# Row maxima of causal attention: two heads in row halves of the array, at the end of each step

## The chip, the core and the metric

The kernel runs on one core of a Trainium2 chip. The metric is the device time of one execution in microseconds (us), as the median of several runs. TensorE multiplies matrices into PSUM (8 banks of 512 fp32 columns for each of 128 partitions), VectorE and ScalarE read PSUM, GpSimd (POOL) works on SBUF alone, and SyncE (SP) issues most DMA transfers. Each engine works through its own queue in order and waits on semaphores.

## The reference

Two layers over x of shape (8, 1024, 256). A layer normalises x, and adds to x the result of causal attention and that of a mixture of 8 experts, of which each token takes two. In the first layer an expert is two matrices with a ReLU between them, in the second a single matrix, and the gates are normalised there.

```python
xn = _layernorm(x, axis=-1)
x = x + _L0_attn_ref(xn, Wq, Wk, Wv, Wo) + _L0_ffn_ref(xn, W_gate, b_gate, W1, b1, W2, b2)
xn = _layernorm(x, axis=-1)
x = x + _L1_attn_ref(xn, Wq, Wk, Wv, Wo, bo) + _L1_ffn_ref(xn, We, be, Wg, bg)
# attention, 16 heads of 16:
scores = jnp.einsum('bhqd,bhkd->bhqk', q, k) / jnp.sqrt(jnp.asarray(HD, x.dtype))
scores = jnp.where(causal, scores, jnp.asarray(-jnp.inf, scores.dtype))
probs = jax.nn.softmax(scores, axis=-1)
out = jnp.einsum('bhqk,bhkd->bhqd', probs, v)
```

The part at stake is the maximum over a row of scores that softmax subtracts before the exponential.

## The kernel before

The work is cut into 16 runs: one layer of one batch each. Batches go in pairs, so that the experts' tiles of one run can be gathered while the other's attention is computed. A run has 48 steps. A step is one unit of attention: a tile of 128 keys against a block of up to 512 queries, for a set of four heads. A run has 8 sets: 4 groups of heads for the first 512 queries (4 steps each), then for the second 512 (8 steps each). All five engines follow the same program of steps, each with its own function `step(g)`, and the order of calls in these functions is the order of work. Tables of step numbers (`TURN`, `PROJ`, `XT`, `VALUES`, `Y`, `GATES` and others) say at which step of a run, or ahead of it, each of the other parts is done. A run's preparation thus goes on while the run before it is at its attention.

Queries and keys are kept as three bf16 parts each (high, middle, low) and a score is the sum of six products of parts, stacked along the rows of one matmul: 6 x 16 = 96 rows. SP loads these stacks from DRAM (`load_stack`, line 457), for queries into `qs`, for keys into `k_first` (first 512 keys) and `k_second`. Two more rows hold the row maxima of the queries, negated and in two bf16 parts, against ones on the key side, so that the score matmul (`scores`, L1147, 98 rows) subtracts them. ScalarE's exponential (`exponentials`, L722) then reads PSUM and writes `probs`, and the attention product (`attend`, L1210) multiplies `probs` with `v`, four heads side by side in column strips of 32, into the bank `po`.

The maxima come ahead, 12 steps before their set's first use at the earliest: `maxima` (L1160) computes scores again, with queries as rows, in pieces of one head, a tile of 128 queries and up to 512 keys, four pieces in every step (`pieces_of`, `maxima_at`). VectorE's `maximum` reduces each piece: a plain maximum where no key lies in the future (L875), a masked one that also takes in the plain piece's result where some do (L879, followed by a read of its accumulator). When all pieces of a set are read, VectorE splits the maxima into two parts (`split_maxima`, L1042 and L1043), TensorE turns them into rows (`turn_maxima`, L1222), VectorE copies these to `mT` (L1049), and SP moves them into the two rows of `qs` (`load_maxima`, L492). `TURN` says at which step.

Two rings of PSUM banks set who waits for whom. The ring `pmx`, 4 banks, takes the pieces of the maxima, the projections of queries and keys (L1290), the output projection (`Y`, L1249), the turned sets and maxima. The ring `pst`, 3 banks, takes the scores, and around them the tokens of an expert's tile (L1168), its hidden layer (L1179, first layer only), its output (L1194), the values (L1301) and the transposes of xn. Each use of a ring takes the next bank and waits until the use before in that bank has been read (`mx_read`, `st_read`). In TensorE's step a piece of the maxima stands ahead of each score:

```python
                for j in range(GH):
                    for piece in work[j:j + 1]:
                        maxima(*piece)
                    if j == 2:
...
                    if j == 3 and tile_out(g):
                        expert_out(*tile_out(g))
                    if unit(g):
                        scores(*unit(g), j)
                    if j == 0 and tile_hidden(g):
                        hidden(*tile_hidden(g))
```

VectorE's step likewise takes the four pieces one by one, with the statistics, the gates and the rest between them. The experts' tiles go through the steps in twos: tokens in odd steps, the output in the next even one (second layer), or hidden layer in the next and the output in the odd step after it (first layer).

## Time and profile before

| what | value |
|---|---|
| runs | 3080.80, 3087.09 and 3089.62 us, median 3087.09 |
| span of the profiled execution | 3081.5 us |
| TensorE (PE) busy | 2982.1 us, 97% |
| VectorE (DVE) busy | 2421.1 us, 79% |
| ScalarE (ACT) busy | 1972.9 us, 64% |
| GpSimd (POOL) busy | 1191.8 us, 39% |
| mean granted TensorE clock | 0.993 |
| DMA | 473.27 MB, mean 154 GB/s |

The span is the time from the first to the last instruction of the profiled execution; it lies among the runs' times, so that nothing of weight stands around it. Busy time counts the time in which at least one instruction of the engine was under way. Matmuls are pipelined: one lasts longer than the distance to the next start, so for TensorE the distances between starts tell more than the durations.

### The profile page before, as it was taken

What the parts mean: (1) busy time and instruction counts of PE and PEld (TensorE: products, weight loads), DVE (VectorE), ACT (ScalarE), POOL (GpSimd) and SP (SyncE); (2) the same over time, 40 slices, a digit from 0 to 9 for tenths busy, and PEclk for the clock granted to TensorE, in tenths of its full rate; (3) what the DMA queues carried; (4) which work ended last, traced back from release to release, by engine and by line L of the source; (5) the groups of instructions that cost most, each with busy time, mean ns of one, the idle gap of its engine ahead of it and who ended that gap; (6) DMA issues with size and microseconds to landing.
All of it is one profiled execution on the core that took longest, in us unless ns stands there. A gap on an engine that the chain in (4) does not pass through costs nothing.

```text
span 3081.5 us, 62739 instructions
## 1 busy us (share of the span) xinstructions
PE 2982.1 (97%) x19312; PEld 1582.3 (51%) x19312; DVE 2421.1 (79%) x7517; ACT 1972.9 (64%) x4954; POOL 1191.8 (39%) x1424
## 2 busy tenths in 40 slices
PE   6999999999999999999999999999999999999998
PEld 3555545444565554545455555454545556544443
DVE  7777788887777878888777887878888777787884
ACT  2666666666666666666666666666666666666665
POOL 3325234252523525335252342534435243252533
PEclk8999999999999999999999999999999999999999
DMA  5766455363655645446374554635547465453642
GB/s 166 208 180 198 133 152 156 109 191 115 187 170 145 178 136 162 132 123 186 110 211 140 166 165 134 176 110 152 178 117 212 138 176 161 126 164 109 170 137 66
DMA packets 276876, 473.27 MB, mean 154 GB/s; under 512 B 52960, under 2 KB 185792, under 8 KB 274496
## 3 DMA queue, kind: packets, MB, share of 16 engines
q1 hardware_dynamic: 236928, 379.48, 40.9%
q0 software_dynamic: 29952, 81.83, 10.2%
q10 hardware_dynamic: 9664, 7.93, 0.9%
q8 instruction: 159, 2.61, 0.4%
q14 instruction: 173, 1.42, 0.2%
HBM read 344.19 MB, written 130.03 MB: 154 GB/s over the span
## 4 chain that ended last, share of the span: by engine, by line
PE 81%; DVE 10%; issue 4%; ACT 3%; POOL 1%; DMA 0%; ACTq 0%; DVEq 0%; POOLq 0%
PE po L1210 17%; PE pmx L1160 15%; PE pst L1147 13%; PE pst L1194 10%; PE pmx L1290 6%; PE pst L1179 5%; DVE pmx L879 4%; PE pst L1301 4%; PE pmx L1249 3%; PE pst L1168 3%; PE pmx L1228 2%; PE pst L1216 2%; DVE rmax L875 1%; ACT probs L722 1%; ACT oraw L751 1%
## 5 line engine op out<-in xcount | busy, mean ns | idle before, releaser
L722 ACT ACTIVATE probs<-pst 128x512 f32<-128x512 f32 (+3 forms) x3072 | 1401.8, 497 | 413.5 <-PE pst L1147 409.7
L621 POOL TENSOR_SCALAR_AFFINE_SELECT probs<-probs 128x512 f32<-128x512 f32 x512 | 326.7, 638 | 1464.7 <-ACT probs L722 1463.6
L875 DVE TENSOR_REDUCE rmax<-pmx 128x1 f32<-128x512 f32 x1024 | 671.1, 683 | 127.6 <-PE pmx L1160 121.0
L1147 PE MATMUL pst<-qs,k_first 98*128 98x512 bf16 (+3 forms) x2048 | 688.6, 342 | 8.7 <-ACT probs L722 4.3
L1160 PE MATMUL pmx<-k_first,qs 96*128 96x512 bf16 (+2 forms) x2048 | 668.0, 343 | 16.1 <-DVE rmax L879 5.0
L879 DVE CUSTOM_DVE_ANT_0 pmx<-pmx,mask,rmax 128x128 f32<-128x128 f32 (+3 forms) x1024 | 534.5, 555 | 162.7 <-PE pmx L1160 152.9
L1210 PE MATMUL po<-probs,v 128*32 128x512 f32 (+3 forms) x6144 | 657.5, 500 | 4.2 <-POOL probs L621 4.1
L879 DVE CUSTOM_DVE_ANT_0 pmx<-pmx,mask 128x128 f32<-128x128 f32 (+3 forms) x1024 | 483.4, 510 | 125.7 <-PE pmx L1160 124.5
L594 POOL DMA_INDIRECT xg<-xn_rows,rows_of x368 | 357.9, 973 | 95.7 <-issue 51.4
L1160 PEld LDWEIGHTS pmx<-k_first,qs 96*128 96x128 bf16 x2048 | 198.6, 98 | 348.0 <-issue 122.5
L1160 PE MATMUL pmx<-k_second,qs 96*128 96x128 bf16 (+3 forms) x1024 | 304.2, 301 | 17.5 <-DVE otok L1016 8.7
L1147 PE MATMUL pst<-qs,k_second 98*128 98x512 bf16 (+3 forms) x1024 | 300.3, 301 | 3.0 <-ACT probs L722 2.2
L608 POOL DMA_INDIRECT yk<-y_slots,slot x256 | 244.9, 957 | 123.2 <-DVE x L1036 46.3
L1147 PEld LDWEIGHTS pst<-qs,k_first 98*128 98x128 bf16 x2048 | 199.5, 98 | 178.0 <-ACT probs L722 50.7
L879 DVE DVE_READ_ACCUMULATOR2_ANT rmax<- 128x1 f32 x2048 | 288.5, 141 | 0.0
L744 ACT ACTIVATE ys<-pst 128x256 f32<-128x256 f32 x368 | 142.8, 388 | 181.1 <-PE pst L1194 137.4
L1290 PE MATMUL pmx<-xnT,wqk 128*128 128x512 f32 x512 | 247.6, 607 | 7.3 <-DVE rmax L875 6.5
L1210 PEld LDWEIGHTS po<-probs,v 128*32 128x32 f32 x6144 | 121.1, 108 | 219.9 <-issue 171.2
L727 ACT ACTIVATE xgT<-pst 128x256 f32<-128x256 f32 x368 | 142.6, 387 | 119.7 <-PE pst L1168 117.2
L627 POOL TENSOR_TENSOR parts<-rest,parts 128x512 bf16<-128x512 f32 x128 | 148.8, 1163 | 178.1 <-ACT parts L766 178.1
L761 ACT ACTIVATE parts<-pmx 128x512 bf16<-128x512 f32 x128 | 76.4, 597 | 191.8 <-PE pmx L1290 191.8
L1194 PE MATMUL pst<-wt,hT 128*128 128x256 f32 x736 | 194.7, 386 | 3.2 <-ACT probs L722 3.2
(143 smaller groups left out, 3626.4 us busy)
## 6 DMA issues: line engine op xcount, KB each, us to landing
wt<-w_tiles SPq DMA_DIRECT2D x161, 513.0 KB
qk_parts<-parts SPq DMA_DIRECT2D x256, 192.0 KB
y_slots<-ys SPq DMA_DIRECT2D x368, 128.0 KB
wt<-w_tiles SPq DMA_DIRECT2D x184, 256.0 KB
qs<-qk_parts SPq DMA_DIRECT2D x128, 192.0 KB
xn_rows<-xn SPq DMA_DIRECT2D x16, 1024.0 KB, 6.4
qs<-qk_parts SPq DMA_DIRECT2D x128, 128.0 KB
k_first<-qk_parts SPq DMA_DIRECT2D x64, 192.0 KB, 3.8
```

The lines of the kernel that those rows point to most:

```text
L594: pool.indirect_dma_start(out=xg[:, m % XRING], out_offset=None, in_=xn_dram[q % 2], in_offset=bass.IndirectOffsetOnAxis(ap=rows_of[:, q % ...
L608: pool.indirect_dma_start(out=yk[:, m % GRING], out_offset=None, in_=y_dram[q % 2], in_offset=bass.IndirectOffsetOnAxis(ap=slot[:, q % 2, ...
L621: pool.affine_select(out=tri, in_=tri, compare_op=ALU.is_ge, fill=0.0, base=0, pattern=[[0, GH], [1, P]], channel_multiplier=-1).then_inc( ...
L722: act.activation(probs[:, u % 2, j, 0:w], ps[:, 0:w], ACT.Exp, scale=DH ** -0.5).then_inc(st_read, 1)
L875: dve.tensor_reduce(rmax0[:, col:col + 1], src, AX_X, ALU.max).then_inc(mx_read, 1)
L879: dve.tensor_tensor_reduce(out=src, in0=src, in1=mask[:, BANK - (b - a):BANK], op0=ALU.add, op1=ALU.max, scale=1.0, scalar=rmax0[:, col:co ...
L1147: pe.matmul(ps[:, 0:w], keys[0:SROWS, j, k % HT * P:(k % HT + 1) * P], qs[0:SROWS, set_no(q, n) % QRING, j, a:a + w], start=True, stop=Tru ...
L1160: pe.matmul(bk[:, 0:b - a], qs[0:STACK, set_no(q, n) % QRING, j, t % HT * P:(t % HT + 1) * P], keys[0:STACK, j, 0:b - a], start=True, stop ...
L1179: mm = pe.matmul(ps[:, j * P:(j + 1) * P], wt[:, m % WRING, a:a + P], xgT[:, m % 2, k], start=(k == 0), stop=(k == KD - 1))
L1194: mm = pe.matmul(ps[:, 0:D], src[:, m % 2, k], wt[:, m % WRING, a:a + D], start=(k == 0), stop=(k == KD - 1))
L1210: mm = pe.matmul(po[HS * j:HS * (j + 1), BANK - w:BANK], v[:, q % 2, k, col:col + HS], probs[:, u % 2, j, 0:w], start=(k == 0), stop=(u in ...
L1290: mm = pe.matmul(ps[:], wqk[l][:, m, k, tile * P:(tile + 1) * P], xnT[:, k, c * BANK:(c + 1) * BANK], start=(k == 0), stop=(k == KD - 1))
```

## The change

In words:

- `pieces_of`: the pieces of a set are listed in another order, two heads beside each other: head 0 with head 2, then head 1 with head 3, the same queries and keys for both; the tiles of queries in the order 0, 3, 1, 2.
- The stacks lie otherwise in `qs`, `k_first` and `k_second`. The four products of high and middle parts (64 rows) lie in rows 0 to 63 for heads 0 and 1 and in rows 64 to 127 for heads 2 and 3; the two products with low parts and the rows of the maxima lie in what is left. The scores of heads 0 and 1 use 98 rows as before, those of heads 2 and 3 use all 128, of which 30 hold zeros.
- `maxima` takes the 64 rows alone, so it leaves the products with low parts out of the maxima, and the two matmuls of a pair use different halves of the array's rows and different banks.
- TensorE's step: all four pieces come last, after the attention product. Projections, values, transposes of xn and output projection now stand after score 0, in place of score 2's turn. VectorE's step: the pieces come last, too. `TURN` is one step later.
- VectorE: `maxima_pair` takes the plain maxima of a pair in one instruction over two neighbouring banks; where the ring's end lies between the two banks, or where there is a mask, `maximum` takes each alone.
- SP: a stack is loaded with six transfers of 32 rows of 2 KB instead of three of 48, 32 and 16 rows of 4 KB; a part is stored with one transfer instead of two. The maxima's rows go two partitions at a time.
- Some memsets for the rows of ones and zeros at the start, and one part of the gates (`GATE_PLACES`) a step earlier.

The diff, cut to its core:

```diff
+MAIN, REST = 4 * DH, 2 * DH
+SIDES = (0, 1), (2, 3)
+MAIN_AT, REST_AT, MAX_AT = (0, P - MAIN), (MAIN, P - MAIN - REST), (STACK, 0)
+SCORE_ROWS = (STACK + MROWS, P)
...
-    return [(j, t, a, min(a + BANK, (t + 1) * P)) for a in range(0, (c + 1) * BANK, BANK)
-            for j in range(GH) for t in range(c * HT, (c + 1) * HT)]
+    return [(side[i], c * HT + t, a, min(a + BANK, (c * HT + t + 1) * P)) for a in range(0, (c + 1) * BANK, BANK)
+            for i in range(len(SIDES[0])) for two in ((0, 3), (1, 2)) for t in two for side in SIDES]
...
-TURN = [MAX0 + (max(i for i, (m, _) in enumerate(PIECES) if m == n) + 1) // PER_STEP for n in range(NSETS)]
+TURN = [MAX0 + 1 + (max(i for i, (m, _) in enumerate(PIECES) if m == n) + 1) // PER_STEP for n in range(NSETS)]
...
+                for side, heads in enumerate(SIDES):
+                    dst = buf[:, heads[0]:heads[-1] + 1].rearrange("p h t -> p (h t)")
+                    for half in range(2):
+                        row = MAIN_AT[side] + half * 2 * DH
+                        two = (src[side, :, 0:2] if m == 0 else
+                               src[side, :, 1 + half].unsqueeze(1).broadcast_to([DH, 2, len(heads) * BANK]))
+                        sp.dma_start(dst[row:row + 2 * DH], two).then_inc(s, 16)
+                    sp.dma_start(dst[REST_AT[side]:REST_AT[side] + REST], src[side, :, 0:3:2]).then_inc(s, 16)
...
+            def maxima_pair(q, n, k):
+
+                j, t, a, b = pieces_of(n)[k]
+                if k == 0 and q * NSETS + n >= 2:
+                    dve.wait_ge(msplit_ready, q * NSETS + n - 1)
+                dve.wait_ge(mx_full, mx_done("max", q, n, k + 1))
+                first = MX["max", q, n, k] % MXRING
+                two = rmax0[:].rearrange("p (j t) -> p j t", t=HT)[:, j::len(SIDES[0]), t % HT]
+                dve.tensor_reduce(two, mx_banks[:, first:first + 2, 0:b - a], AX_X, ALU.max).then_inc(mx_read, 2)
...
-                pe.matmul(bk[:, 0:b - a], qs[0:STACK, set_no(q, n) % QRING, j, t % HT * P:(t % HT + 1) * P],
-                          keys[0:STACK, j, 0:b - a], start=True, stop=True).then_inc(mx_full, 1)
+                main = slice(MAIN_AT[j // len(SIDES[0])], MAIN_AT[j // len(SIDES[0])] + MAIN)
+                pe.matmul(bk[:, 0:b - a], qs[main, set_no(q, n) % QRING, j, t % HT * P:(t % HT + 1) * P],
+                          keys[main, j, 0:b - a], start=True, stop=True).then_inc(mx_full, 1)
...
             def step(g):
-                work = maxima_at(g)
                 if tile_turned(g):
                     turn_tokens(*tile_turned(g))
                 for j in range(GH):
-                    for piece in work[j:j + 1]:
-                        maxima(*piece)
-                    if j == 2:
+                    if j == 3 and tile_out(g):
+                        expert_out(*tile_out(g))
+                    if unit(g):
+                        scores(*unit(g), j)
+                    if j == 0:
+                        if tile_hidden(g):
+                            hidden(*tile_hidden(g))
...
+                if unit(g - 1):
+                    attend(*unit(g - 1))
+                for piece in maxima_at(g):
+                    maxima(*piece)
```

How this moves instructions. On TensorE, before, around a step of the second layer with unmasked maxima and the end of its set (po is the attention product, pst from qs a score, pmx from qs a piece of the maxima, pst from wt an expert's output, pmx from mparts the turn of the maxima):

```order
L1210 MATMUL po<-probs,v 32x256 x4
L1160 MATMUL pmx<-k_first,qs 128x512
L1147 MATMUL pst<-qs,k_first 128x512
L1160 MATMUL pmx<-k_first,qs 128x512
L1147 MATMUL pst<-qs,k_first 128x512
L1160 MATMUL pmx<-k_first,qs 128x512
L1147 MATMUL pst<-qs,k_first 128x512
L1160 MATMUL pmx<-k_first,qs 128x512
L1194 MATMUL pst<-wt,xgT 128x256 x2
L1147 MATMUL pst<-qs,k_first 128x512
L1222 MATMUL pmx<-identb,mparts 128x128
L1210 MATMUL po<-probs,v 32x128 x4
```

The same step with the change, and the start of the next (L1174 is a score, L1188 a piece of the maxima, L1222 now the expert's output, L1238 the attention product, L1196 the tokens):

```order
L1174 MATMUL pst<-qs,k_first 128x512 x3
L1222 MATMUL pst<-wt,xgT 128x256 x2
L1174 MATMUL pst<-qs,k_first 128x512
L1238 MATMUL po<-probs,v 32x128 x4
L1188 MATMUL pmx<-k_first,qs 128x512 x4
L1196 MATMUL pst<-ident,xg 128x128 x2
```

The three first scores now follow each other, the four pieces stand in a row behind the attention product, and the turn of the maxima has left this step for the next.

On VectorE, before, at the end of a set's pieces (L879 is the masked piece and the read of its accumulator, L1042 and L1043 the split, L875 a plain piece of the next set, L852 and L855 statistics, L1049 the copy of the turned maxima):

```order
L879 ISA pmx,rmax<-pmx,mask,rmax 128x384
L879 ISA rmax 128x1
L879 ISA pmx,rmax<-pmx,mask,rmax 128x512
L879 ISA rmax 128x1
L1042 TENSOR_SCALAR mparts<-rmax 128x16
L1043 SCALAR_TENSOR_TENSOR mparts<-rmax,mparts 128x16
L875 TENSOR_REDUCE rmax<-pmx 128x1 x2
L852 BN_STATS stats<-x 128x6 x2
L855 BN_AGGR mv<-stats 128x2 x2
L875 TENSOR_REDUCE rmax<-pmx 128x1 x2
L1049 COPY mT<-pmx 32x128
```

With the change (L885 the masked piece, L858 and L861 the statistics, L898 a pair of plain pieces, L1065 and L1066 the split, L1034 to L1037 the result of a turned set, L1072 the copy):

```order
L885 ISA pmx,rmax<-pmx,mask,rmax 128x384
L885 ISA rmax 128x1
L885 ISA pmx,rmax<-pmx,mask,rmax 128x384
L885 ISA rmax 128x1
L858 BN_STATS stats<-x 128x6 x2
L861 BN_AGGR mv<-stats 128x2 x2
L898 TENSOR_REDUCE rmax<-pmx 128x2 x2
L1065 TENSOR_SCALAR mparts<-rmax 128x2x8
L1066 SCALAR_TENSOR_TENSOR mparts<-rmax,mparts 128x2x8
L1034 TENSOR_SCALAR osum<-pmx 128x16
L1035 RECIPROCAL osum<-osum 128x16
L1037 TENSOR_TENSOR otok<-pmx,osum 128x4x64
```

The split of a set now stands behind the pieces of the next set's first step, and the statistics ahead of them.

## Rows read from the trace of the kernel before

**Rows 1.** The page, busy times of the engines (us, share of the span, instructions).

```profile
PE 2982.1 (97%) x19312; PEld 1582.3 (51%) x19312; DVE 2421.1 (79%) x7517; ACT 1972.9 (64%) x4954; POOL 1191.8 (39%) x1424
```

**Rows 2.** The page, chain that ended last, share of the span by line.

```profile
PE po L1210 17%; PE pmx L1160 15%; PE pst L1147 13%; PE pst L1194 10%; PE pmx L1290 6%; PE pst L1179 5%; DVE pmx L879 4%; PE pst L1301 4%; PE pmx L1249 3%; PE pst L1168 3%; PE pmx L1228 2%; PE pst L1216 2%; DVE rmax L875 1%; ACT probs L722 1%; ACT oraw L751 1%
```

**Rows 3.** Order of time, TensorE in a dense step: start us, us it lasts, instruction.

```profile
1363.51 0.22 PE L1160 MATMUL pmx<-k_second,qs 96*128 96x128 bf16 x1
...
1364.50 0.38 PE L1160 MATMUL pmx<-k_second,qs 96*128 96x512 bf16 x1
1364.72 0.38 PE L1147 MATMUL pst<-qs,k_first 98*128 98x512 bf16 x1
1365.03 1.06 PE L1210 MATMUL po<-probs,v 128*32 128x512 f32 x8
1366.03 0.23 PE L1160 MATMUL pmx<-k_first,qs 96*128 96x128 bf16 x1
```

**Rows 4.** Groups by line and form, the attention product: count, busy us, mean ns.

```profile
L1210 PE MATMUL po<-probs,v 128*32 128x512 f32 x3072 | 411.7, 608 | 0.1
```

**Rows 5.** Order of time, TensorE and ScalarE in the last run's last steps.

```profile
3034.90 0.82 PE L1147 MATMUL pst<-qs,k_second 98*128 98x512 bf16 x3
...
3036.12 1.10 PE L1194 MATMUL pst<-wt,xgT 128*128 128x256 f32 x4 [0.41 <-ACT probs L722]
...
3049.05 0.82 PE L1147 MATMUL pst<-qs,k_first 98*128 98x512 bf16 x3
...
3049.54 2.07 ACT L722 ACTIVATE probs<-pst 128x512 f32<-128x512 f32 x4 [0.66 <-PE pst L1147]
...
3050.19 0.39 PE L1147 MATMUL pst<-qs,k_first 98*128 98x512 bf16 x1 [0.32 <-ACT probs L722]
```

**Rows 6.** Order of time, tokens of an expert's tile and the first exponential.

```profile
3032.11 0.44 PE L1168 MATMUL pst<-ident,xg 128*128 128x128 f32 x2
...
3032.58 0.38 ACT L727 ACTIVATE xgT<-pst 128x256 f32<-128x256 f32 x1 [0.65 <-PE pst L1168]
...
3032.91 0.60 ACT L722 ACTIVATE probs<-pst 128x512 f32<-128x512 f32 x1
```

**Rows 7.** Groups by line and form, projections.

```profile
L1290 PE MATMUL pmx<-xnT,wqk 128*128 128x512 f32 x512 | 247.6, 607 | 7.3 <-DVE rmax L875 6.5 <-DVE rmax L879 0.2
...
L1249 PE MATMUL pmx<-wo,attn 128*128 128x256 f32 x512 | 129.9, 382 | 0.0
```

**Rows 8.** Stretches: length, busy us by engine, granted clock, DMA share, GB/s.

```profile
1306.00:1350.10 44.10, 41.78 (x247) 19.77 (x246) 37.87 (x114) 24.67 (x59) 13.02 (x15) 0.96 0.40 106
...
3049.00:3060.50 11.50, 9.91 (x65) 2.34 (x62) 4.21 (x9) 9.05 (x20) 7.03 (x8) 1.00 0.24 69
```

**Rows 9.** Order of time, VectorE at four masked pieces and the split.

```profile
3032.64 0.36 DVE L879 CUSTOM_DVE_ANT_0 pmx<-pmx,mask,rmax 128x128 f32<-128x128 f32 x1 [1.71 <-PE pmx L1160]
...
3033.92 0.76 DVE L879 CUSTOM_DVE_ANT_0 pmx<-pmx,mask,rmax 128x512 f32<-128x512 f32 x1
3034.59 0.14 DVE L879 DVE_READ_ACCUMULATOR2_ANT rmax<- 128x1 f32 x1
3034.77 0.17 DVE L1042 TENSOR_SCALAR mparts<-rmax 128x16 bf16<-128x16 f32 x1
3034.97 0.17 DVE L1043 SCALAR_TENSOR_TENSOR mparts<-rmax,mparts 128x16 bf16<-128x16 f32 x1
```

**Rows 10.** Groups by line and form, VectorE's plain maximum.

```profile
L875 DVE TENSOR_REDUCE rmax<-pmx 128x1 f32<-128x512 f32 x1024 | 671.1, 683 | 127.6 <-PE pmx L1160 121.0
```

**Rows 11.** Waits of TensorE's weight loads: us in total, times, longest.

```profile
PEld pmx L1160 <- DVE rmax L879: 119.8, 202, 1.2
...
PEld pst L1147 <- ACT probs L722: 65.2, 181, 0.9
PEld pmx L1160 <- DVE rmax L875: 47.5, 89, 0.8
```

**Rows 12.** Order of time, SP issues the three transfers of a stack.

```profile
1501.81 1.31 SPq L464 DMA_DIRECT2D k_second<-qk_parts  x3
```

**Rows 13.** Waits of SP's queue: us in total, times, longest.

```profile
SPq L525 <- ACT ys L744: 813.2, 208, 8.0
```

More of the change, by code:

```diff
@@ L219, in uses @@
             mx["rows", q] = len(mx)
+        for q, n, k in maxima_at(g):
+            mx["max", q, n, k] = len(mx)
     return mx, st
@@ L1099, in step @@
                     take_rows(q)
+                work = maxima_at(g)
+                for i in range(0, len(work), 2):
+                    if in_pair(*work[i]):
+                        maxima_pair(*work[i])
+                    else:
+                        maximum(*work[i])
+                        maximum(*work[i + 1])
             def order_weights(l):
```

155 lines of the change are left out of this document (70 added, 85 removed).

## The prediction

> **What bounds the kernel now.** I read the page's busy times first, then the chain that ended last, then the order of time in a dense stretch and in the last steps, then the waits. TensorE is busy 97% of the span and VectorE 79% [rows 1]; line L1160, the maxima matmuls, is 15% of the chain, second to the attention product [rows 2]. So TensorE's own queue sets the end, and what counts is how far apart its matmuls start. In a dense step [rows 3] the reader is to see the starts: from the first maxima matmul at 1363.51 to the last score at 1364.72 stand four maxima (128, 256, 384 and 512 columns) and three scores of 512; a 512 takes 0.22 us to the next start, so the four maxima take 1.21 - 3 x 0.22 = 0.55 us. The attention product starts 0.31 us after the last score instead of 0.22, so entering its 32-column strips costs 0.09, and the next matmul starts 1.00 us after it.
>
> There are 16 runs of 48 steps, 768 in all, with four maxima matmuls in each. In 256 steps all four have 512 columns and no mask (4 x 0.22 = 0.88 us), in 512 they are the masked row of rows 3 (0.55): together 225 + 282 = 507 us of TensorE's time.
>
> **The change, part by part.** The sum is made against the profiled span, 3081.5 us; the runs took 3080.8 to 3089.6, with a median 5.6 above the span, which I add at the end. About 0.3% (9 us) is what a measurement of this kernel can tell from no change.
>
> *Pairs.* Two heads' maxima now use rows 0 to 63 and 64 to 127 of the array, one right behind the other, in two banks. No row of before shows two matmuls on different rows. The nearest is the attention product: eight matmuls of 512 columns in 1.00 us [rows 3], though each lasts 0.608 [rows 4]; they run four at a time in four column strips. Bounds: nothing gained, if the halves take turns, or half of 507, 253 us. I take 253, since that row shows tiles at work side by side. The Trainium skill, TensorE: Matmul & The Clock Gate, section Measured speedup vs the span model, gives 3.07 times for four row tiles of 512 columns; an estimate from it for two is 1.53 times, so 176 us, and the sum would be 77 us higher. No run here shows it yet.
>
> *One more change of tiling a step.* The maxima follow the attention product, so the way out of its strips leads into row halves, and a way from these to whole rows is new. Bounds: 0, or the entry's 0.09. I take 0.09 x 768 = 69 us.
>
> *Scores in a burst.* This is the dearest part. Before, a maxima matmul stood between each two scores; now at most an expert's tile does, and the ring pst still has three banks: score 3 needs the bank of score 0, which ScalarE must have read. The last twelve steps of before have no maxima left and show just this [rows 5]: three scores start from 3049.05 on, the fourth could at 3049.71 (3 x 0.22), but the first exponential starts at 3049.54 and the fourth score at 3050.19, 0.48 us late. With the expert's output in fourth place (3034.90, then 3036.12) it is 0.56. With token tiles ahead [rows 6] ScalarE starts the first exponential 0.80 us after the tokens and needs 0.60; the fourth score could start at 0.27 + 3 x 0.22 = 0.93 and starts at 1.40, again 0.47. Only where a projection (247.6 us in 128 steps, 1.9 each) or an output projection (129.9 in 64, 2.0 each) stands between the first two scores [rows 7] is there no wait. That leaves 36 of 48 steps: 576 x 0.48 = 276 us. Bounds: 0.40 each, 230, if steps with values or token transposes between the scores wait less, and 0.56 each, 323. The clock adds nothing: over those bursts the granted clock is 1.00, the 2.4 GHz level [rows 8].
>
> *VectorE later by most of a step.* Its maxima can't begin before TensorE's last matmuls of a step. Four masked pieces take it from 3032.64 to 3034.59, 1.95 us, and the split of the maxima ends 0.55 later [rows 9]. Two unmasked pieces in one instruction cost between one reduce, 0.68, and two, 1.37 [rows 10]; from the masked forms (0.76 for 512 columns, 0.36 for 128 [rows 9], so 1.04 ns a column) I take 0.68 + 0.53 = 1.21. What that saves VectorE in 385 pairs (the ring's end keeps 127 apart) lies in its idle time: 0 on the path. But a finished set's split stands behind the maxima of the next set's first step, so it is ready 2.5 to 2.9 us after TensorE finished those, while TensorE's turn of it (L1222) stands behind the scores alone, some 1.7 us after. In a quarter of the 128 turns nothing else stands between (no expert's output, no set), and TensorE waits some 0.95; in the others some 0.15: 32 x 0.95 + 96 x 0.15 = 45 us. Likewise 64 output projections and 32 projections of layer 1 that follow an unmasked step ask for the first pair's bank 0.3 to 0.6 us after it was written, and it is free after 1.21: 0.6 each, 55 us. Bounds of both together: 0 and 200.
>
> *Waits of before that go.* TensorE's weight loads waited 119.8 and 47.5 us for VectorE's maxima and, at the scores, 65.2 for ScalarE [rows 11]; such a wait is partly covered by the matmul in flight. TensorE's own idle time is 99 us in all (span less busy, [rows 1]), start and end included. Between 60 and 230 I take 110 as lost time that the new order replaces.
>
> *Edits at nothing.* SP issues six transfers per stack instead of three, 768 more at 0.44 each (three in 1.31 us [rows 12]), 340 us, less 128 stores; it waits 813 us for ScalarE at L525 [rows 13], which covers that. Without this cover a stack would come 1.3 us later, and it is loaded several steps ahead. The split's rows reach qs a step later; three steps remain. The wider memsets cost a few us at the start at most.
>
> The sum: -253 + 69 + 276 + 45 + 55 - 110 = +82. From 3081.5 that is 3163.5, and with 5.6 for the median 3169.
>
> **The rivals.**
> *Faster: one wait covers the other.* While TensorE waits for ScalarE in each burst, VectorE catches up; then its waits of before vanish as far as the weight loads' rows say (200 us) and turns and banks cost nothing: -253 + 69 + 276 - 200 = -108, so 2979. For it: VectorE has only 79%. Against it: the waits at turns and banks run from the end of the maxima, whatever came before. It decides from where VectorE's side, waits gone less waits new, reaches 92 us.
> *VectorE becomes the bound.* In the ten steps with the gates (1306.0 to 1350.1) VectorE is busy 37.87 of 44.10 us [rows 8]. If it must stand idle there each time until the step's last matmuls, some 0.6 us in each of 160 steps, 96 us come on top: 3265. Against it: TensorE's steps get longer too. The Trainium skill, TensorEngine Tiling (Array Packing), section PSUM Bottleneck, says that tiling speeds up TensorE but not the emptying of PSUM, which may then be the bottleneck; these rows neither bear it out nor exclude it.
> *The halves take turns.* Then the 253 us aren't gained: 3422. For it: no row shows row halves. Against it: the column strips do run together.
>
> **How the numbers follow.** Forecast 3169, from 3100 to 3240: 0.45. Within 0.3% of before, between it and the faster rival: 0.06. Faster: 0.24. VectorE the bound: 0.15. Halves in turn: 0.10. So faster 0.24, same 0.06, slower 0.70. The range leaves out the halves in turn and the lower part of the faster case, and holds the rest: 2990 to 3300.
>
> **What would show it.** Right: two maxima matmuls that start almost together, and the next pair 0.22 us later; about 0.09 us lost behind them; the fourth score some 0.48 us late, with the exponential named as what ended the wait; small waits at the maxima. Wrong: 0.22 us between all starts of the maxima line (halves in turn), a fourth score on time, or VectorE without idle time in the gate steps.

## The result and the profile after

The changed kernel takes 3384.14 us (median of 4 runs, 3380.42 to 3389.01) against 3085.03 for the kernel before on the same chip: 1.097 times as long, 95% interval 1.0953 to 1.0987. The forecast was 3169, range 2990 to 3300. The direction was right, the size was not.

Lines have moved: maxima L1160 is now L1188, scores L1147 L1174, attention product L1210 L1238, an expert's output L1194 L1222, tokens L1168 L1196, the turn L1222 L1250, set L1228 L1256, projections L1290 L1318, output projections L1246 and L1249 L1274 and L1277; VectorE's plain maxima are L881 (alone) and L898 (pairs), the masked ones L885.

The page of the changed kernel, busy times, then the chain by engine and by line:

```profile
PE 3010.2 (89%) x19312; PEld 1429.6 (42%) x19312; DVE 2349.0 (69%) x7135; ACT 1951.0 (58%) x4954; POOL 1190.3 (35%) x1426
...
PE 68%; ACT 12%; DVE 12%; issue 6%; DMA 1%; POOL 0%; SPq 0%; ACTq 0%; DVEq 0%; POOLq 0%
PE po L1238 16%; PE pst L1222 10%; PE pmx L1188 9%; PE pst L1174 9%; PE pmx L1318 7%; PE pst L1207 4%; ACT probs L731 4%; DVE rmax L898 3%; PE pmx L1277 3%; PE pst L1196 3%; PE pst L1329 3%; DVE pmx L885 2%; ACT xgT L736 2%; PE pmx L1256 2%
```

The chain by engine before was:

```profile
PE 81%; DVE 10%; issue 4%; ACT 3%; POOL 1%; DMA 0%; ACTq 0%; DVEq 0%; POOLq 0%
```

TensorE was busy 97% of a shorter span [rows 1]; now it is 89%, and VectorE and ScalarE have less to do and yet hold a larger part of the chain, ScalarE above all. The maxima have fallen from 15% [rows 2] to 9%. So TensorE waits. The order of time of two steps without sets or projections shows where (start us, us it lasts, instruction; in brackets the engine's idle time ahead of it and what ended it), TensorE first, then ScalarE:

```profile
1490.34 0.45 PE L1188 MATMUL pmx<-k_second,qs 64*128 64x256 bf16 x4
1490.72 0.82 PE L1174 MATMUL pst<-qs,k_first 98*128 98x512 bf16 x3
1491.95 1.10 PE L1222 MATMUL pst<-wt,xgT 128*128 128x256 f32 x4 [0.41 <-ACT probs L731]
1492.89 0.38 PE L1174 MATMUL pst<-qs,k_first 128*128 128x512 bf16 x1
...
1494.19 0.45 PE L1188 MATMUL pmx<-k_second,qs 64*128 64x128 bf16 x4
1494.57 0.44 PE L1196 MATMUL pst<-ident,xg 128*128 128x128 f32 x2
1494.85 1.52 PE L1174 MATMUL pst<-qs,k_first 98*128 98x512 bf16 x4
1496.29 1.07 PE L1238 MATMUL po<-probs,v 128*32 128x512 f32 x8
```

```profile
1491.21 1.57 ACT L731 ACTIVATE probs<-pst 128x512 f32<-128x512 f32 x3 [0.92 <-PE pst L1174]
...
1495.05 0.38 ACT L736 ACTIVATE xgT<-pst 128x256 f32<-128x256 f32 x1 [1.02 <-PE pst L1196]
1495.33 2.06 ACT L731 ACTIVATE probs<-pst 128x512 f32<-128x512 f32 x4
```

The expert's output is due at 1490.72 + 3 x 0.22 = 1491.38 and starts at 1491.95, 0.57 late, because it needs the bank of score 0, whose exponential began at 1491.21. In the next step four scores behind tokens take 1.44 us (1494.85 to 1496.29) to the attention product instead of 0.97, which is 4 x 0.22 and the 0.09 of its strips. Those are the waits that the prediction read from the last steps of before [rows 5, 6].

The row halves do what the prediction expected of them. Four maxima, a pair of 128 and a pair of 512 columns, take 1494.57 - 1494.19 = 0.38 us, where four with the same number of columns in all took 0.55 [rows 3]. Four of 512 take 0.53, from the first here to the tokens behind them, where the prediction counted 0.88 for the kernel before:

```profile
1011.64 0.61 PE L1188 MATMUL pmx<-k_first,qs 64*128 64x512 bf16 x4
1012.17 0.33 PE L1196 MATMUL pst<-ident,xg 128*128 128x128 f32 x1
```

Over the whole run the two matmuls of an undisturbed pair start 3 to 4 ns apart and the next pair follows 0.222 us behind a pair of 512. Two such matmuls thus take what one did, 0.222 us against 2 x 0.216 in whole rows, 1.95 times as fast. The estimate of 1.53 times, worked out from the Trainium skill (TensorE: Matmul & The Clock Gate, section Measured speedup vs the span model), is too low for a row of pairs.

A second kind of wait was not in the sum. This is step 25 of a run of the second layer, TensorE and then VectorE:

```profile
1448.77 0.66 PE L1256 MATMUL pmx<-ident,oraw 128*128 128x128 f32 x4
1449.35 1.06 PE L1238 MATMUL po<-probs,v 128*32 128x512 f32 x8
1450.35 0.44 PE L1188 MATMUL pmx<-k_second,qs 64*128 64x256 bf16 x3
1452.60 0.33 PE L1188 MATMUL pmx<-k_second,qs 64*128 64x384 bf16 x1 [1.80 <-DVE otok L1037]
...
1454.09 2.04 PE L1222 MATMUL pst<-wt,xgT 128*128 128x256 f32 x4 [0.21 <-ACT probs L731]
```

```profile
1448.66 0.22 DVE L932 TENSOR_TENSOR equal<-equal,countdown 128x64 f32<-128x64 f32 x1
...
1449.42 1.14 DVE L936 SCALAR_TENSOR_TENSOR others<-chosen,gs 128x64 f32<-128x64 f32 x1
...
1451.37 0.22 DVE L943 TENSOR_REDUCE gtot<-equal 128x8 f32<-128x64 f32 x1
1451.62 0.17 DVE L1034 TENSOR_SCALAR osum<-pmx 128x16 f32<-128x16 f32 x1
...
1452.12 0.42 DVE L1037 TENSOR_TENSOR otok<-pmx,osum 128x256 f32<-128x256 f32 x1
```

A set is written at 1448.77, and with the four maxima it makes five uses of a ring of four banks: the fourth maximum needs the set's bank. VectorE has eight instructions of the gates in front of its read of that bank, 1448.66 to 1451.62, and TensorE stands for 1.80 us. Half of this is particular to the step: L936 lasted 1.14 us, where its median over 16 executions is 0.23, while GpSimd's L634 ran beside it from 1449.31 to 1450.48. Stretched instructions are not what the change added: where one of VectorE's lasts over 0.15 us longer than the median of its form, the excess sums to 52 us here and to 81 in the kernel before. After the wait TensorE's clock falls (windows: length, busy us by engine, granted clock, DMA share, GB/s), and the expert's output lasts 2.04 us instead of 1.10:

```profile
1446.00:1452.60 6.60, 4.55 (x35) 1.52 (x34) 5.50 (x21) 4.37 (x10) 2.85 (x3) 1.00 0.32 85
1452.60:1456.00 3.40, 3.19 (x9) 1.62 (x9) 3.23 (x16) 1.57 (x3) 0.24 (x1) 0.61 0.85 270
```

To sum such waits over a run I took every distance between starts of neighbouring matmuls, grouped by the two lines, the shape and the place among the maxima. The tenth percentile of a group counts as undisturbed; what a distance has above it (over 30 ns) is a wait, put to the engine that the trace names; for the rest of the waits it names another engine or none. A wait that nearly all of a group share is thus in the undisturbed part, and a stretch at the lower clock counts among the waits. The last column is the mean granted clock of the profiled run. In us:

| kernel | time | undisturbed | waits | for ScalarE | for VectorE | clock |
|---|---|---|---|---|---|---|
| before | 3085 | 2855 | 189 | 70 | 71 | 0.993 |
| changed | 3384 | 2738 | 605 | 384 | 146 | 0.988 |
| changed order, whole rows | 3452 | 2860 | 553 | 395 | 97 | 0.993 |
| changed, short exponentials | 3285 | 2734 | 505 | 238 | 176 | 0.991 |
| changed, short maxima | 3241 | 2698 | 502 | 371 | 62 | 0.993 |
| changed order, whole rows, short maxima | 3336 | 2836 | 463 | 373 | 27 | 0.994 |
| maxima mid-step, projections last, halves | 3252 | 2771 | 435 | 74 | 228 | 0.978 |
| the same, whole rows | 3239 | 2855 | 343 | 61 | 182 | 0.986 |
| before, gates in lumps | 3130 | 2855 | 235 | 67 | 106 | 0.988 |

From before to changed, 117 us of TensorE's own time went and 416 us of waits came; 299 is the difference of the times. The clock has a small part in it: the span times what its mean lacks to 1 is 22 us before, 24 in the changed order with whole rows and 41 in the changed kernel. The clock's own cost can be no more than that.

### The profile page after: what moved, and what is told of

The parts are those of the page before. It is cut to its first block, busy times and chain, and to the rows that moved or that the text cites. A ratio compares the mean times of both kernels' runs of the same rounds, so it can differ in the third digit from the quotient of the medians.

```text
span 3381.6 us, 63229 instructions
## 1 busy us (share of the span) xinstructions
PE 3010.2 (89%) x19312; PEld 1429.6 (42%) x19312; DVE 2349.0 (69%) x7135; ACT 1951.0 (58%) x4954; POOL 1190.3 (35%) x1426
## 3 DMA queue, kind: packets, MB, share of 16 engines
q14 instruction: 176, 1.44, 0.1%
## 4 chain that ended last, share of the span: by engine, by line
PE 68%; ACT 12%; DVE 12%; issue 6%; DMA 1%; POOL 0%; SPq 0%; ACTq 0%; DVEq 0%; POOLq 0%
PE po L1238 16%; PE pst L1222 10%; PE pmx L1188 9%; PE pst L1174 9%; PE pmx L1318 7%; PE pst L1207 4%; ACT probs L731 4%; DVE rmax L898 3%; PE pmx L1277 3%; PE pst L1196 3%; PE pst L1329 3%; DVE pmx L885 2%; ACT xgT L736 2%; PE pmx L1256 2%; ACT hT L744 2%
## 5 line engine op out<-in xcount | busy, mean ns | idle before, releaser
L731 ACT ACTIVATE probs<-pst 128x512 f32<-128x512 f32 (+3 forms) x3072 | 1361.0, 496 | 619.3 <-PE pst L1174 603.7
L1174 PE MATMUL pst<-qs,k_first 128*128 128x512 bf16 (+7 forms) x2048 | 615.1, 345 | 79.3 <-ACT hT L744 19.6
L885 DVE CUSTOM_DVE_ANT_0 pmx<-pmx,mask,rmax 128x128 f32<-128x128 f32 (+3 forms) x1024 | 504.9, 555 | 250.1 <-PE pmx L1188 249.6
L1238 PE MATMUL po<-probs,v 128*32 128x512 f32 (+3 forms) x6144 | 657.7, 500 | 3.5 <-POOL probs L628 3.5
L885 DVE CUSTOM_DVE_ANT_0 pmx<-pmx,mask 128x128 f32<-128x128 f32 (+3 forms) x1024 | 471.6, 523 | 194.8 <-PE pmx L1188 191.4
L898 DVE TENSOR_REDUCE rmax<-pmx 128x2 f32<-128x1024 f32 x385 | 458.9, 1220 | 170.7 <-PE pmx L1188 169.3
L1174 PEld LDWEIGHTS pst<-qs,k_first 98*128 98x128 bf16 (+1 forms) x2048 | 194.5, 97 | 398.7 <-issue 101.7
L1188 PE MATMUL pmx<-k_first,qs 64*128 64x512 bf16 (+3 forms) x2048 | 308.0, 344 | 13.4 <-DVE rest L1079 5.0
L885 DVE DVE_READ_ACCUMULATOR2_ANT rmax<- 128x1 f32 x2048 | 289.7, 141 | 0.0
L1318 PE MATMUL pmx<-xnT,wqk 128*128 128x512 f32 x512 | 255.6, 623 | 33.4 <-DVE rmax L898 16.7
L1174 PE MATMUL pst<-qs,k_second 98*128 98x512 bf16 (+7 forms) x1024 | 251.2, 303 | 31.3 <-ACT xgT L736 10.9
L1222 PE MATMUL pst<-wt,xgT 128*128 128x256 f32 x736 | 204.1, 400 | 43.7 <-ACT probs L731 32.0
L1222 PE MATMUL pst<-wt,hT 128*128 128x256 f32 x736 | 202.2, 397 | 37.0 <-ACT probs L731 12.0
L1188 PEld LDWEIGHTS pmx<-k_first,qs 64*128 64x128 bf16 x2048 | 76.7, 94 | 366.6 <-issue 203.6
L634 POOL TENSOR_TENSOR parts<-rest,parts 128x512 bf16<-128x512 f32 x128 | 148.4, 1159 | 196.1 <-ACT parts L775 196.1
L881 DVE TENSOR_REDUCE rmax<-pmx 128x1 f32<-128x512 f32 x254 | 162.9, 683 | 59.5 <-PE pmx L1188 59.5
```

The source lines that it names most:

```text
L731: act.activation(probs[:, u % 2, j, 0:w], ps[:, 0:w], ACT.Exp, scale=DH ** -0.5).then_inc(st_read, 1)
L885: dve.tensor_tensor_reduce(out=src, in0=src, in1=mask[:, BANK - (b - a):BANK], op0=ALU.add, op1=ALU.max, scale=1.0, scalar=rmax0[:, col:co ...
L898: dve.tensor_reduce(two, mx_banks[:, first:first + 2, 0:b - a], AX_X, ALU.max).then_inc(mx_read, 2)
L1174: pe.matmul(ps[:, 0:w], keys[0:rows, j, k % HT * P:(k % HT + 1) * P], qs[0:rows, set_no(q, n) % QRING, j, a:a + w], start=True, stop=True) ...
L1188: pe.matmul(bk[:, 0:b - a], qs[main, set_no(q, n) % QRING, j, t % HT * P:(t % HT + 1) * P], keys[main, j, 0:b - a], start=True, stop=True) ...
L1222: mm = pe.matmul(ps[:, 0:D], src[:, m % 2, k], wt[:, m % WRING, a:a + D], start=(k == 0), stop=(k == KD - 1))
```

## The experiments

**The order without the halves.** The stacks of before (96 rows for each maximum), with their transfers, under the changed order of all engines. The line at the core of it:

```diff
-                main = slice(MAIN_AT[j // len(SIDES[0])], MAIN_AT[j // len(SIDES[0])] + MAIN)
+                main = slice(0, STACK)
```

> The changed order of work on all engines (maxima last in each step, the pair instruction, a turn a step later) with the stacks of before: all 96 rows for every maxima matmul, so two heads' matmuls follow one another. Theory of waits (the loss is in the order, and the halves gain what was predicted): TensorE has 253 us more matmul time and 69 us less drain, some 185 us more; up to half of it falls into its present waits for VectorE and ScalarE, so 3384 + 90 to 185: 3475 to 3570. Rival (row halves gain little or nothing beside each other, and the loss is theirs): within 40 us of the changed kernel, 3345 to 3425, or faster.

It took 3452.34 us, ratio 1.1195 [1.1176, 1.1214]. The order alone costs 367 us, and the halves give back 68. That lies between the two, 23 us under the theory's range and 27 over the rival's. The burst stands there unchanged; four scores behind tokens again take 1.45 us to the attention product:

```profile
1515.93 0.72 PE L1175 MATMUL pmx<-k_second,qs 96*128 96x128 bf16 x4
1516.49 0.38 PE L1183 MATMUL pst<-ident,xg 128*128 128x128 f32 x2
1516.71 1.52 PE L1161 MATMUL pst<-qs,k_first 98*128 98x512 bf16 x4
1518.16 1.06 PE L1225 MATMUL po<-probs,v 128*32 128x512 f32 x8
```

**Short exponentials, in both kernels.**

```diff
-                act.activation(probs[:, u % 2, j, 0:w], ps[:, 0:w], ACT.Exp, scale=DH ** -0.5).then_inc(st_read, 1)
+                act.activation(probs[:, u % 2, j, 0:64], ps[:, 0:64], ACT.Exp, scale=DH ** -0.5).then_inc(st_read, 1)
```

> The changed kernel, but each exponential reads and writes 64 columns of its score bank instead of 128 to 512; the rest of the probabilities is left out. ScalarE's exponential of 512 columns (0.60 us) then takes some 0.2 us, and the bank of score 0 is free before score 3 wants it. Burst theory (most of the loss is TensorE waiting for ScalarE to empty three score banks; the trace of the changed kernel has about 380 us of such waits, before about 70): 3384 - 250 to 300, so 3080 to 3130. Bank theory (most of the loss is the fourth bank of the maxima, which VectorE empties late because a set's, a turn's or a projection's bank stands ahead of it): at most 120 us off, 3260 to 3380, since VectorE's stretch of the step is as long as it was and takes the place of the waits removed.

> The same cut of the exponentials (64 columns, the rest left out) in the kernel before, as the control. There a maxima matmul stands between the scores and the trace has about 70 us of waits for ScalarE. Burst theory: 3085 - 30 to 70, so 3015 to 3055, a fifth of what the changed kernel gains. If both kernels gain alike, the burst is not what the change costs.

They took 3284.71 (1.0659 [1.064, 1.0677]) and 3047.43 (0.9882 [0.9866, 0.9899]): 99 us gained against 37. The first is in the bank theory's range and far from the burst theory's, the control is in the range named for it. But 238 us of waits for ScalarE remain, since its other copies out of the same ring (tokens, hidden layer, values, transposes) are as long as they were, and VectorE's waits grow by 30: the cut was no clean measure of the burst.

**Short maxima, in both kernels.** For the pairs, and likewise in the plain and the masked pieces:

```diff
-                dve.tensor_reduce(two, mx_banks[:, first:first + 2, 0:b - a], AX_X, ALU.max).then_inc(mx_read, 2)
+                dve.tensor_reduce(two, mx_banks[:, first:first + 2, 0:P], AX_X, ALU.max).then_inc(mx_read, 2)
```

> The changed kernel, but VectorE's maxima read only 128 columns of each bank (the masked ones the last 128, the plain ones the first); the other columns are left out of the maxima, so a row's shift is smaller than its true maximum. VectorE's part falls from 1.22 us a pair to some 0.35, from 0.36 to 0.76 a masked piece to 0.36. Bank theory: the waits at the maxima, the sets, the turns and the projections go, about 290 us by the trace (VectorE 179, and 111 that the trace puts down to no one): 3384 - 150 to 250, so 3130 to 3230. Burst theory: TensorE then waits for ScalarE where it waited for VectorE, at most 100 us off: 3280 or more.

> The same cut of VectorE's maxima (128 columns, the others left out) in the kernel before, as the control. The trace of before has about 72 us of waits for VectorE. Bank theory: 3085 - 40 to 80, so 3005 to 3045. If it gains as much as the changed kernel does, VectorE's lateness is not what the change made.

They took 3240.92 (1.0513 [1.0496, 1.0531]) and 3029.37 (0.9828 [0.9812, 0.9845]): 143 us against 55, just short of the bank theory's 150 to 250 in the changed kernel, and in its range in the other. VectorE's lateness is worth 88 us more in the changed kernel than before.

**The same cut without the halves.** The edit of the first group (whole rows) and the one above (128 columns) together.

> The changed order with the whole-row stacks of before (3452), with VectorE's maxima cut to 128 columns of each bank (the others left out of the maxima). The same cut made the changed kernel with its row halves 3241. Theory V (the halves save the predicted 180 us of TensorE's time, and VectorE's lateness takes most of it back: 68 us are left of it): with VectorE early the halves gain 110 to 160, so this kernel is at 3350 to 3400. Rival T (the halves themselves cost TensorE more than the pairs and drains counted): they gain some 70 as before, so 3290 to 3330.

It took 3336.11 (1.082 [1.08, 1.0839]): with VectorE early the halves gain 95 us, between the two theories and nearer to T. Undisturbed distances differ by 138 (2836 against 2698), the waits give back 39, the start is 4 us later. So neither theory holds alone: the halves cost TensorE more than counted, and VectorE takes back a part.

**VectorE's split a step earlier.**

```diff
-                for n, q in at_step(g, TURN):
+                for n, q in at_step(g + 1, TURN):
                     split_maxima(q, n)
```

> The changed kernel with VectorE's split of a finished set's maxima one step earlier: ahead of the next set's first maxima instead of behind them. TensorE's turn waits 37 us for the split in the trace of the changed kernel (and 5 more that are put down to nobody). Theory of the late split: 3384 - 30 to 45, so 3339 to 3354. Rival (the wait only moves to the next bank or the next exponential): within 10 us, 3374 to 3394.

It took 3350.32 (1.0858 [1.0837, 1.0878]), 34 us less, as the theory has it.

**VectorE reads all banks ahead of the gates.** The reads of projections, output projections, sets and turns move from behind statistics, combining and gates to a place ahead of them:

```diff
                 for n, q in at_step(g, TURN):
                     split_maxima(q, n)
+                for (c, n), q in at_step(g, PROJ):
+                    split_projection(q, c, n)
...
+                for n, q in at_step(g, TURN):
+                    turn_maxima(q, n)
...
                 for c in range(CH):
                     for a, q in at_step(g, STATS[c]):
                         statistics(q, c, a)
```

> The changed kernel with VectorE's order inside a step turned: it empties the banks of projections, output projections, sets and turns first and does the statistics, the gates and the combining behind them, ahead of the maxima as before. Theory of the fourth bank (a maximum asks for the bank of the set, turn or projection of its own step, which VectorE empties late because gates and statistics stand ahead): the waits of the maxima for these banks, 40 + 26 + 17 us and part of the 72 that are put down to nobody, go: 3384 - 60 to 120, so 3264 to 3324. Rival (VectorE is simply full in those steps, and what it does later is waited for instead): within 15 us.

It took 3485.97 (1.1312 [1.1291, 1.1333]), 102 us more: a miss. With the projection's read in front, VectorE now stands still until ScalarE has copied the projection (217.1 us at L1079 by the first line, 102.3 in the changed kernel), and the gates and all banks behind them come later; output projections alone wait up to 4.3 us, by the second line (us in total, times, longest). The mean granted clock sinks from 0.988 to 0.975.

```profile
L1079 DVE TENSOR_TENSOR rest<-pmx,parts 128x512 f32<-128x512 f32 x128 | 88.5, 692 | 218.2 <-ACT parts L770 217.1
...
PE pmx L1274 <- DVE rmax L898: 81.5, 48, 4.3
```

**Set and turn behind the maxima.** TensorE, and VectorE's reads likewise:

```diff
                 for piece in maxima_at(g):
                     maxima(*piece)
+                for q, n in set_ended(g):
+                    turn_set(q, n)
+                for n, q in at_step(g, TURN):
+                    turn_maxima(q, n)
```

> The changed kernel with a set's and a turn's transposes behind the maxima on TensorE, and VectorE's reads of them behind its maxima: no bank of a set or a turn stands between the maxima of its own step any more, and the turn comes 1.5 us later than the split it waits for. Theory of the same-step bank and the late split: of the waits of the changed kernel 20 (set's bank), 13 (turn's bank), 37 (split) and 16 us (a set for ScalarE's copy of it) go, and the burst stays: 3384 - 60 to 100, so 3284 to 3324. Rival (VectorE's queue as a whole is late, whatever the banks' order): within 25 us of 3384.

It took 3456.99 (1.122 [1.1201, 1.1239]), 73 us more, another miss. The fifth use of the ring waits wherever it stands close to the maxima: now it is the set that waits for the first maximum's bank. TensorE's order of time, and the sum of such waits (us in total, times, longest):

```profile
1410.84 0.45 PE L1188 MATMUL pmx<-k_second,qs 64*128 64x256 bf16 x4
1411.85 0.63 PE L1256 MATMUL pmx<-ident,oraw 128*128 128x128 f32 x4 [0.57 <-DVE rmax L885]
```

```profile
PE pmx L1256 <- DVE rmax L885: 62.0, 93, 2.0
```

**Maxima between the second and the third score.** TensorE's part of the edit; VectorE's order follows it, and `TURN` is a step earlier:

```diff
                     if unit(g):
                         scores(*unit(g), j)
+                    if j == 1:
+                        for piece in maxima_at(g):
+                            maxima(*piece)
...
-                for piece in maxima_at(g):
-                    maxima(*piece)
```

> The maxima stand between the second and the third score instead of last; VectorE empties them behind the projections' banks and ahead of gates, sets and turns, and a set is turned one step earlier again. A step has one more change of tiling (0.09 us, 69 us in all) but no burst of four scores, and no set or turn between two banks of the maxima is waited for in its own step. Theory of burst and banks: of some 700 us of TensorE's waits about 400 to 500 go, and 69 come: 3384 - 330 to 430, so 2955 to 3055, faster than both kernels. Rival (the changes of tiling cost more than 0.09 each, or VectorE's time is the bound): 3150 or more.

It took 3356.13 (1.0884 [1.0866, 1.0902]). Waits for ScalarE fell from 384 to 102 us, so the burst is what made most of them. The time is in the rival's range, yet for another reason: each of 124 projections, written ahead of the maxima in the same step, now holds the fourth maximum up (us in total, times, longest):

```profile
PE pmx L1189 <- DVE rest L1080: 120.3, 124, 1.9
```

**The same with projections at the end of the step.**

```diff
                 for _, q in at_step(g, [INVERSE]):
                     find_rows(q)
+                for (c, n), q in at_step(g, PROJ):
+                    project(q, c, n)
+                for b, q in at_step(g, Y):
+                    project_output(q, b)
                 if unit(g - 1):
                     attend(*unit(g - 1))
```

> The kernel with the maxima between the second and third score (3356), whose trace has 167 us of waits of the maxima for the bank of a projection and 57 for that of an output projection, both written ahead of them in the same step: here projections and output projections stand at the end of the step, ahead of the attention product, with ScalarE's and VectorE's reads of them behind those of the exponentials and of the set. Theory of the same-step bank: these 223 us go, some 30 come back elsewhere: 3356 - 160 to 220, so 3136 to 3196. Rival (VectorE is full in the steps with gates, and waits only move): 3280 or more.

It took 3251.66 (1.0553 [1.0536, 1.0571]), between the two: 104 of the 160 to 220 us, so part of the waits moved. In the step shown first for the changed kernel the output now starts 0.31 us behind the third score, where it was 0.79:

```profile
1435.98 0.60 PE L1175 MATMUL pst<-qs,k_first 98*128 98x512 bf16 x2
1436.51 0.45 PE L1189 MATMUL pmx<-k_second,qs 64*128 64x128 bf16 x4
1436.89 0.39 PE L1175 MATMUL pst<-qs,k_first 128*128 128x512 bf16 x1
1437.20 1.10 PE L1223 MATMUL pst<-wt,xgT 128*128 128x256 f32 x4
1438.14 0.38 PE L1175 MATMUL pst<-qs,k_first 128*128 128x512 bf16 x1
```

**That order with whole rows, and with short maxima.** The edits of the first and the third group on top of it.

> The order with the maxima between the second and third score and the projections at the end of the step, as in the run at 3252, with the whole-row stacks of before. There is one change of tiling more in a step with halves than in the changed kernel. Theory V (there, too, VectorE's lateness takes back part of what the halves save): halves gain 30 to 110, this kernel 3280 to 3360. Rival (the burst of scores was the only loss, and the halves pay in full without it): 180 less 69 and more, 3360 to 3430. If it is faster than 3240, the halves cost here.

> The run at 3252 with VectorE's maxima cut to 128 columns of each bank. Its trace has 228 us of waits for VectorE and some 35 us more of a low clock than before. Theory V: 130 to 200 of it go, 3050 to 3120. Rival (other waits, for ScalarE and GpSimd, take their place): 3150 or more. The kernel before with the same cut took 3029.

They took 3238.97 (1.0508 [1.0486, 1.0531]) and 3065.37 (0.994 [0.9921, 0.9959]). In this order the halves cost 13 us, which neither theory had (the last sentence of the first text names the case): they save 84 us of undisturbed time, 71 more being lost on the way from the scores into the halves, and waits grow by 92. Some of these 92 are the clock's, at most 26: with the halves its mean is 0.978, without them 0.986, which makes 71 and 45 us of the two spans. Whole rows against whole rows, this order is worth 3452 - 3239 = 213 us; the burst is taken apart in it, but the projections, the turns and VectorE's reads have moved, too. And 186 us of the halves' version hang on how soon VectorE empties the banks, as theory V has it.

**Projections ahead of the last score.** VectorE reads all banks in TensorE's order, the gates behind; a second kernel has the gates ahead of sets and turns.

```diff
                     if j == 3 and tile_out(g):
                         expert_out(*tile_out(g))
+                    if j == 3:
+                        for (c, n), q in at_step(g, PROJ):
+                            project(q, c, n)
+                        for b, q in at_step(g, Y):
+                            project_output(q, b)
                     if unit(g):
                         scores(*unit(g), j)
```

> Maxima between the second and third score as in the run at 3252, whose trace has waits of the maxima for the banks of a projection (60 us), a set (27) and a turn (15). Here projections and output projections stand right ahead of the last score, with ScalarE's copy of them ahead of its last exponential, and VectorE reads all banks in the order in which TensorE fills them, with statistics, gates and combining behind them. Theory of the same-step banks: these 102 us go, and some 20 come at the projections: 3252 - 60 to 100, so 3150 to 3190. Rival (VectorE is full in the steps with gates; its lateness only moves): 3230 or more. Faster than the kernel before only if still more goes.

> As the kernel beside it, but VectorE does statistics, gates and combining ahead of its reads of sets and turns again (behind the projections). Theory of the same-step banks: the waits for sets and turns, some 40 us, are back: 20 to 60 us more than the kernel beside it. Rival (VectorE's queue as a whole decides): within 15 us of it.

They took 3369.12 (1.0924 [1.0902, 1.0945]) and 3353.63 (1.0871 [1.0853, 1.089]), 117 and 102 us worse than with the projections at the end, and the second, which was to be the slower one, is 15 us faster; the theory fell with both: waits only moved, to output projections, the scores and the causal mask, and the granted clock sank to 0.971 over the first of them (0.978 with the projections at the end, 0.988 in the changed kernel, 0.993 before).

**Gates in lumps, in the kernel before.**

```diff
-                            if q is not None and place_at % 4 == m:
+                            if q is not None and m == 3:
                                 gates(q, part)
```

> The kernel before with one thing changed: in the steps with gates, VectorE does all parts of the gates of a step in one go behind the step's last piece of maxima, instead of one part behind each piece. Nothing else of the order moves and no work is added. Theory of lumps (VectorE has the time, but a bank of the maxima ring must not lie behind three or four parts of the gates in its queue): its waits rise in the 160 steps with gates by 0.2 to 0.5 us each, so 3085 + 30 to 80: 3115 to 3165. Rival (VectorE is late in these steps only because it is full): within 10 us of 3085.

It took 3130.01 (1.0156 [1.0135, 1.0177]), 48 us more with the same work, as the theory of lumps has it. At most some 16 of these are the clock's, whose mean falls from 0.993 to 0.988. The change does much the same to VectorE's queue: up to five parts of the gates in one go, ahead of the step's other reads, where one stood behind each piece before.

None of the kernels that leave nothing out beats the kernel before.

## Why the prediction was wrong in size

The direction and the two mechanisms, pairs in row halves and a burst of scores, were right. Two steps of the sum failed. The halves' net gain, -253 + 69 = -184, was taken in full as time off the kernel, and 68 us of it were left. The new order's waits were put at 276 + 45 + 55 - 110 = 266 us, and the order alone cost 367. Term by term:

- **Pairs, -253: right.** Between the changed kernel and its order with whole rows the distances within the maxima shrink by 149 + 102 = 251 us.
- **One more change of tiling, +69: right, with an addition.** The distances from the last maximum to tokens and scores grow by 34 + 37 = 70 us, 0.31 us instead of 0.22 behind 512 columns. Not foreseen: the tokens' second transpose starts 0.16 us after the first one, with whole rows in the same order 0.11, which is 19 us in 368 tiles. It was 0.16 in the kernel before, too, behind the strips of the attention product; so the order alone would have gained these 19 us, and the halves take them back.
- **Scores in a burst, +276: the mechanism right, the size short.** Waits for ScalarE rise by 325 us in the order alone and by 313 in the changed kernel. 585 steps have no projection or output projection, and each waits 0.62 us rather than 0.48, above the upper bound of 0.56: some 363 us where 276 were put. The last steps of before, from which 0.48 was read, hold only tokens and outputs; with one of these alone the changed kernel waits 0.55 to 0.59, with both some 0.74. With a set and tokens the wait is about 0.75 to 1.15, with transposes of xn some 0.65: ScalarE's copies of these stand between the exponentials in its queue, so the banks come free later still. The estimate left them out.
- **Turns and banks, +45 and +55: right for the turns** (37 us by the trace, 34 by the run with an earlier split); at projections and output projections the waits rise from 24 to 54 us, so by 30 where 55 were put.
- **Waits of before that go, -110: not borne out.** VectorE's waits are 71 us before, 97 in the order alone and 146 with the halves. Those ahead of the maxima themselves, without turns and projections, are about 50, 35 and 70 us, so few of them went. The traces show five uses of four banks within a step, with lumps of the gates ahead of VectorE's read. Runs that moved a set or a projection inside the step moved the wait with it; one that only lumps the gates adds 48 us to the kernel before. How the 101 us that the order cost beyond its sum divide between this term and the burst stays open: the 110 held waits for ScalarE, too, which the sums here can't part from the burst's.
- **The halves' net gain, -253 + 69 = -184: measured 68; this is the largest miss.** Undisturbed distances shrink by 122 only: the tokens' 19 come on top, 27 between the first score and projections or output projections, most of which ask for a bank that VectorE has not yet read (with short maxima these are 12), and small ones. The waits take 52 (605 less 553), the start 4. VectorE's waits rise by 49 (97 to 146); up to 17 of the 52 are the clock's (41 less 24).

Together: 266 was put for the order's waits and 367 was measured, 101 more; 184 for the halves and 68, 116 less. 82 + 101 + 116 = 299. The edits put at nothing stayed there: waits for transfers are 4 us, and the wider memsets start TensorE 4 us later. The clock, put at nothing, takes at most 19 us more than before (41 less 22).

The rival in which one wait covers the other (2979) fell: waits for VectorE grew beside those for ScalarE. The rival of a full VectorE (3265) put 96 us on the steps with gates, and the traces don't show that much: of the ten steps that the prediction counts in each run, nine hold parts of the gates before and eight in the changed kernel; the thirteen steps from the first of them on became 7.0 us longer on average, but any thirteen steps became 4.9 us longer, so these stand out by some 2 us in a run, 34 in all. VectorE is busy 69%, and the lumps alone cost 48 us in a kernel whose VectorE had no more work, so its order counts, not only its load. The Trainium skill, TensorEngine Tiling (Array Packing), section PSUM Bottleneck, says that tiling speeds up TensorE but not the emptying of PSUM, which may then become the bottleneck. The runs agree in part: short maxima, with which VectorE empties the banks sooner, raise the halves' gain from 68 to 95 us, not to 184, and up to 14 of these 27 us come through the clock (17 us more with the halves at full maxima, 3 with short ones). Halves in turn (3422) gives a time nearer to the measured one than the forecast does, but by chance: it is refuted by the starts, 3 to 4 ns apart. How much of VectorE's waits is load and how much is order in the changed kernel itself was not tried apart.

## What to carry to other kernels

When an order of work changes, count for each ring of buffers the uses between one that is read late and the next that needs its bank, and everything that its reader has queued ahead, copies for other work included. Read the price of a burst from steps of every kind, not from the emptiest ones. Time saved on an engine that waits for two others may be given back to them: here 184 us became 68, and in another order -13.

## What was not expected of the hardware

- Two matmuls of 64 rows and 512 columns on different halves of the rows start 3 to 4 ns apart and the next pair follows after 0.222 us, so a pair costs what one matmul did.
- Leaving the halves for whole rows costs 0.09 us (0.31 between starts behind 512 columns instead of 0.22), and of a pair of fp32 transposes right behind them the second comes 0.05 us later (0.16 instead of 0.11), as it did behind the 32-column strips before. Coming into the halves from these strips costs no more than into whole rows (0.525 us from the last product of 512 columns in both).
- A single wait of 1.80 us was followed by a stretch at a mean granted clock of 0.61, that is largely at the lower of the two levels, 1.2 GHz; four matmuls then took 2.04 us instead of 1.10. All ten falls of the clock in the changed kernel between 112 and 3109 us stand behind a wait of TensorE of 1.5 to 2.6 us.
- An instruction of VectorE that takes 0.23 us (median of 16) lasted 1.14 us, from 1449.42 to 1450.56, while one of GpSimd's was under way from 1449.31 to 1450.48.
